# Graph attention in a network kernel: the value product also gives the weight sums, VectorE multiplies the edge counts in on the way out of PSUM, and GpSimd forms the exponential product

## Chip, cores and metric

One core of one Trainium2 chip. The metric is the device time of the kernel in microseconds (us), taken as the median of several runs. The profile shows one execution, instruction by instruction; its times are counted from the start of its span.

## What is computed

The reference applies eight blocks to 625 nodes of 512 features each. The change touches only the first, a graph attention with 8 heads of 64 features over 10,000 edges:

```python
score = s_src + s_dst + einsum(diff, a_dif) + einsum(abs(diff), a_abs) + einsum(hr_src * hr_dst, a_prd)
alpha = leaky_relu(score, negative_slope=0.2)
ex = exp(alpha.T - segment_max(alpha.T, src)[src])
att = ex / (segment_sum(ex, src)[src] + 1e-16)
out = segment_sum(att[:, :, None] * h_e[:, dst], src)      # one row per node, 8 heads x 64
x = x + out
```

The kernel treats the edges as a dense 625 x 625 matrix for each head. An entry that has several edges is weighed by their number (`CNT`), an entry without an edge by zero.

## The kernel before

The 625 nodes are 5 tiles of 125. The stage in question takes 5 tiles x 8 heads, so 40 heads `k = 8 t + h`, and for each it makes the 125 x 625 block of weights of the tile's source nodes against all nodes. Each engine has its own order of instructions, written out by hand, and semaphores tie them together. There are four buffers `SP0[k % 4]` for the block and four `BENT[k % 4]` for its second exponential; the PSUM tile `RAW` of raw scores and the PSUM tile `TURNED` exist once.

One head goes through these steps (names are functions of the program; one line number each, of the main instruction):

- `raw(k)`, TensorE (L946, L948): the raw scores into `RAW`, as a piece of 512 columns in one bank and one of 113 (114) in the next. It waits until VectorE has read `RAW` for head k-1.
- `raw_scores(k)`, VectorE (L2387): adds the edge term `TSC`, writes `SP0` and takes the row maximum. `shift(k)` (L2396, L2398) makes the biases of the exponentials of it.
- `bent(k)` (L1652) and `exp_scores(k)` (L1658, L1659), ScalarE: the leaky rectifier is split, so that the weight is the product of two exponentials, "slope" in `SP0` and "bend" in `BENT`.
- `counted(k)`, GpSimd (L1994): multiplies the slope exponential by `CNT`.
- `weighted(k)`, VectorE (L2406): multiplies by the bend exponential and sums each row, which gives the denominator.
- `turn_head(k)`, TensorE (L958): 5 transposes into `TURNED`. `turned_head(k)`, ScalarE (L1663): copies them to `PTS`.
- the value product, TensorE (L981): 5 fp32 matmuls (10 entries in the trace) of `PTS` with 64 columns of `HE`, into a PSUM slot "N" that holds all 8 heads of the tile.

TensorE's order in round k is `raw(k+4)`, `left` when k % 4 == 1 (L930: 8 matmuls that make the left factor of the next four heads, in a PSUM slot "T"), `turn_head(k+1)`, value product of head k. VectorE's is `left` when k % 4 == 3 (L2377), `raw_scores(k+4)`, `weighted(k+2)`, `shift(k+4)`, in the first rounds `merge` (L2308, L2309: two adds of 125 x 625 that complete `CNT` and `G` of a tile, at k = 1 and 6), and at h == 2 `add_heads(t-1)` for the tile before: denominator and reciprocal (L2414, L2415), multiply out of PSUM (L2417), add to X (L2422), statistics (L2099 to L2101), and the normalisation of the tile before that (L2106). Below, a round is the time from one `raw_scores` to the next.

SyncE loads the edge terms of tile t+1 (2.4 MB) into `TSC` once the tile t-1 has been read. After the last tile the normalised rows are turned (L735) and the next block starts (L996).

Of the kernel before, what the change touches and what calls it, by code (L numbers as in the profile page):

```python
# [21 lines left out]
N, E, D = 625, 10000, 512  # L22
P, NT = 125, 5
# [11 lines left out]
MAIN, TAIL = BANK, N - BANK  # L35
MAGIC = 12582912.0
# [148 lines left out]
def program(nc, a, out, loops):  # L185
# [6 lines left out]
    def passing(name, shape, dt=F32):  # L192

        with nc.sbuf_tensor(name, shape, dt) as t:
            return t
# [11 lines left out]
    with ctx:  # L207
# [20 lines left out]
        EA1 = passing("EA1", [DH0, N])  # L228
        CONDR = sb("CONDR", [128, N], F32R)
# [46 lines left out]
        HR_ = 5072  # L276
# [4 lines left out]
        with nc.sbuf_tensor("AR_hot", [128, 10192], F32):  # L281
            HOT1 = passing("HOT1", [128, NT, 4 * P], F32R)
# [21 lines left out]
        HE = XL  # L304
# [10 lines left out]
        IDB = [view(12696 + 1000 * b, 128, 2, 1000, dt=I16) for b in range(2)]  # L315
# [27 lines left out]
        SUMS_AT = [YF, AR[:, PT_:PT_ + 2500], AR[:, PT_ + 2500:PT_ + 5000], YF, YF]  # L343
# [23 lines left out]
        TSC = [view(at, P, N * HEADS0) for at in (HR_ + 2 * NT * D, PT_)]  # L367
# [3 lines left out]
        PTS = [view(HR_ + 2 * NT * D + 5000 + 625 * b, P, NT, P) for b in range(2)]  # L371
        SG = [view(PT_ + 625 * b, 128, N) for b in range(2)]
# [32 lines left out]
        RAW = PS[0:P, 2 * BANK:2 * BANK + N + 1]  # L405
# [35 lines left out]
        counted_ready = sem("counted_ready")  # L441
        heads_turned, heads_taken = sem("heads_turned"), sem("heads_taken")
        negmax_ready, exp_ready, sums_ready = sem("negmax_ready"), sem("exp_ready"), sem("sums_ready")
        weights_summed, prob_ready = sem("weights_summed"), sem("prob_ready")
# [20 lines left out]
        normed_before = []  # L465
# [229 lines left out]
        def _(pe):  # L695
# [81 lines left out]
            pe.wait_ge(start_done, 9)  # L777
# [182 lines left out]

# [5 lines left out]
            for k in range(4):  # L966
                raw(k)
            turn_head(0)
            for k in range(HEADS_ALL):
                h = k % HEADS0  # L970
                if k + 4 < HEADS_ALL:
                    raw(k + 4)
                if k % 4 == 1:
                    left((k + 7) // 4)
                if k + 1 < HEADS_ALL:
                    turn_head(k + 1)
                if h == 0:
                    o = fill("N")
                pe.wait_ge(heads_taken, k + 1)
                for c in range(NT):  # L980
                    last = mm(o.ap[0:P, DH0 * h:DH0 * (h + 1)], PTS[k % 2][:, c, :],  # L981
                              HE[:, c, DH0 * h:DH0 * (h + 1)], start=(c == 0), stop=(c == NT - 1))
                if h == HEADS0 - 1:
                    last.then_inc(o.filled, 1)
            pe.wait_ge(raw_taken, HEADS_ALL)
# [482 lines left out]
        def _(act):  # L1468
# [58 lines left out]
            act.wait_ge(start_done, 9)  # L1527
            act.wait_ge(keys_ready, 2)
            for t in range(NT):
                if t == NT - 1:  # L1530
                    psum.skip(T=ET // 4, W=STEPS - 1)
                    s = take("W")
                    fn(NODE_ROWS, s.ap[0:96, 0:N], ACT.Copy)
                    fn(VROW[:, :], s.ap[0:96, 0:N], ACT.Copy).then_inc(s.taken, 1)
                    act.wait_ge(s.taken, n.now(s.filled))
                    psum.skip(W=1)
                s = take("N")
                fn(HE[:, t, :], s.ap[0:P, :], ACT.Copy).then_inc(s.taken, 1)
                if t < 4:
                    apart(t)  # L1540
                    from_hot(t)
# [105 lines left out]
            def bent(k):  # L1647
                t, h = divmod(k, HEADS0)
                act.wait_ge(raw_taken, k + 1)
                if k >= 4:  # L1650
                    act.wait_ge(weights_summed, k - 3)
                fn(BENT[k % 4], SP0[k % 4], ACT.Relu, bias=U[:, t, h:h + 1]).then_inc(bent_ready, 1)  # L1652
# [21 lines left out]
            turned_head(0)  # L1674
            for k in range(HEADS_ALL):
                if k + 3 < HEADS_ALL:
                    exp_scores(k + 3)
                if k + 1 < HEADS_ALL:
                    turned_head(k + 1)
# [4 lines left out]
            psum.skip(N=NT)  # L1684
# [238 lines left out]
        def _(pool):  # L1923
# [12 lines left out]
            g.memset(SM[:, :], 0.0).then_inc(start_done, 1)  # L1936

# [52 lines left out]
            def counted(k):  # L1990
                if k % HEADS0 == 0:
                    pool.wait_ge(sums_merged, k // HEADS0 + 1)
# [3 lines left out]
            for k in range(3):  # L1996
                counted(k)
            for k in range(NT * HEADS0):
                t, h = divmod(k, HEADS0)
                if k + 3 < NT * HEADS0:  # L2000
                    counted(k + 3)
                if h == 2 and t:
                    inverse_roots([t - 1])
# [69 lines left out]
        def _(dve):  # L2073
# [65 lines left out]
            dve.wait_ge(start_done, 9)  # L2139
# [160 lines left out]
            dve.wait_ge(start_done, 9)  # L2300
# [100 lines left out]
            def weighted(k):  # L2401
                t, h = divmod(k, HEADS0)
                z = SP0[k % 4]
                dve.wait_ge(bend_ready, k + 1)
                dve.wait_ge(counted_ready, k + 1)
# [4 lines left out]
            def add_heads(t):  # L2410

                den = HM[:, t % 2, 3, :]
                dve.wait_ge(weights_summed, HEADS0 * (t + 1))
                step(v.tensor_scalar(den, HM[:, t % 2, 2, :], 1e-16, None, ALU.add))  # L2414
                step(v.reciprocal(den, den))  # L2415
                s, y = take("N"), Y[0:P, t, :]
                v.tensor_tensor(y.rearrange("p (h d) -> p h d", d=DH0),  # L2417
                                s.ap[0:P, :].rearrange("p (h d) -> p h d", d=DH0),
                                den.unsqueeze(2).broadcast_to([P, HEADS0, DH0]), ALU.mult)\
                 .then_inc(s.taken, 1)  # L2420
                dve.wait_ge(s.taken, n.now(s.filled))
                step(v.tensor_tensor(X[0:P, t, :], X[0:P, t, :], y, ALU.add))  # L2422
                stats(t, X[0:P, t, :])
                if t:
                    norm_y(t - 1)
# [11 lines left out]
            weighted(0)  # L2437
            weighted(1)
            for k in range(NT * HEADS0):
                t, h = divmod(k, HEADS0)  # L2440
                if k % 4 == 3:
                    left((k + 5) // 4)
                if k + 4 < NT * HEADS0:
                    raw_scores(k + 4)
                if k + 2 < NT * HEADS0:
                    weighted(k + 2)
                if k + 4 < NT * HEADS0:
                    shift(k + 4)
                if k in (1, 6):
                    merge(3 + k // 6)  # L2450
                if h == 2 and t:
                    add_heads(t - 1)
            add_heads(NT - 1)
# [571 lines left out]
```

## Time and profile before

| what | us |
|---|---|
| median of 3 runs (2321.63 to 2322.45) | 2321.89 |
| span of the profiled execution | 2314.6 |
| the attention stage in it, first `raw_scores` to the last value product | 173.3 |
| TensorE busy over the span | 2155.4 |
| VectorE busy over the span | 1043.3 |

The profiled execution's span ends with its last instruction; the 7.3 us between it and the median of the runs lie around it. PE is TensorE's matmul queue, PEld its weight loads, DVE VectorE, ACT ScalarE, POOL GpSimd, SP SyncE. A busy PE in the profile is not a PE at its peak: ends of matmuls are modelled, and neighbouring ones overlap, so the pace is read from starts. PEclk is the granted TensorE clock, 1.00 for 2.4 GHz and 0.50 for 1.2 GHz.

### The profile page before, as it was taken

What the parts mean: (1) busy time and instruction counts of PE and PEld (TensorE: products, weight loads), DVE (VectorE), ACT (ScalarE), POOL (GpSimd) and SP (SyncE); (2) the same over time, 40 slices, a digit from 0 to 9 for tenths busy, and PEclk for the clock granted to TensorE, in tenths of its full rate; (3) what the DMA queues carried; (4) which work ended last, traced back from release to release, by engine and by line L of the source; (5) the groups of instructions that cost most, each with busy time, mean ns of one, the idle gap of its engine ahead of it and who ended that gap; (6) DMA issues with size and microseconds to landing.
All of it is one profiled execution on the core that took longest, in us unless ns stands there. A gap on an engine that the chain in (4) does not pass through costs nothing.

```text
span 2314.6 us, 21913 instructions
## 1 busy us (share of the span) xinstructions
PE 2155.4 (93%) x8137; PEld 1248.1 (54%) x8137; DVE 1043.3 (45%) x2156; ACT 729.8 (32%) x1221; POOL 540.3 (23%) x457
## 2 busy tenths in 40 slices
PE   6899896888889999988999999999999999999998
PEld 3566563787445555444565565565555544444443
DVE  8897677886324332454454453453453410000002
ACT  1576555675421110003243243243242111111110
POOL 4677762332210000110202202202202200022202
PEclk9999998787999979998999999999999899999999
DMA  9522205431020110023101101101101577787832
GB/s 344 167 31 38 27 4 126 123 78 58 0 96 19 55 55 7 1 76 116 65 9 59 64 10 59 65 10 59 55 1 55 195 272 297 296 306 294 298 143 71
DMA packets 61507, 237.47 MB, mean 103 GB/s; under 512 B 23343, under 2 KB 28419, under 8 KB 39276
## 3 DMA queue, kind: packets, MB, share of 16 engines
q1 hardware_dynamic: 31898, 168.25, 20.3%
q0 software_dynamic: 26336, 62.19, 8.8%
q10 hardware_dynamic: 3168, 5.63, 0.7%
q8 instruction: 66, 1.08, 0.2%
q14 instruction: 39, 0.32, 0.0%
HBM read 204.06 MB, written 31.96 MB: 102 GB/s over the span
## 4 chain that ended last, share of the span: by engine, by line
PE 68%; DVE 11%; issue 8%; PEld 4%; ACT 3%; DMA 3%; POOL 3%; SPq 0%; PEldq 0%; ACTq 0%; DVEq 0%; POOLq 0%
PE PS L996 10%; PE PS L724 10%; PE PS L717 7%; PE PS L1387 7%; PE PS L1396 7%; PE PS L1425 6%; PE PS L868 3%; PE PS L1293 3%; PE PS L1034 2%; PE PS L1273 2%; PE PS L735 1%; DMA pair_scores<-TS,SIDX 1%; PEld PS L717 1%; DVE AR L2406 1%; POOL pair_scores L1971 1%
## 5 line engine op out<-in xcount | busy, mean ns | idle before, releaser
L1942 POOL TENSOR_TENSOR RSTD<-VE,HALF 125x1 f32<-125x1 f32 x100 | 81.7, 817 | 1017.3 <-DVE VE L2101 1017.3
L996 PE MATMUL PS<-XT,WR 128*128 128x500 f32 (+2 forms) x992 | 236.2, 396 | 8.4 <-ACT XT L1493 4.4
L868 PE MATMUL PS<-HR,HOT 125*125 125x512 f32 x800 | 212.8, 414 | 16.4 <-DVE HOT L2245 16.4
L724 PE MATMUL PS<-WR,XT 128*125 128x512 f32 (+1 forms) x464 | 208.0, 596 | 12.2 <-DVE AR L2696 7.7
L2911 DVE TENSOR_TENSOR AR<-AR,PS 128x512 f32<-128x512 f32 (+1 forms) x44 | 30.2, 687 | 404.9 <-PE PS L1396 404.9
L996 PEld LDWEIGHTS PS<-XT,WR 128*128 128x128 f32 x992 | 146.0, 194 | 89.2 <-issue 74.7
L868 PEld LDWEIGHTS PS<-HR,HOT 125*125 125x125 f32 x800 | 147.9, 193 | 58.5 <-DVE HOT L2245 16.8
L1960 POOL DMA_INDIRECT pair_sums<-CW,SIDX x80 | 136.2, 1703 | 56.3 <-DMA pair_sums<-CW,SIDX 24.5
L724 PEld LDWEIGHTS PS<-WR,XT 128*125 128x125 f32 x464 | 87.1, 194 | 101.4 <-issue 86.4
L717 PE MATMUL PS<-XT,WR 128*128 128x113 f32 (+3 forms) x432 | 127.5, 453 | 1.8 <-DVE CW L2209 1.3
L1902 ACT ACTIVATE AR<-PS 128x512 f32<-128x512 f32 (+1 forms) x44 | 26.3, 597 | 299.3 <-PE PS L1387 299.3
L2123 DVE TENSOR_TENSOR AR<-PS,AR 125x512 f32<-125x512 f32 x55 | 38.0, 691 | 178.7 <-PE PS L724 106.3
L717 PEld LDWEIGHTS PS<-XT,WR 128*128 128x128 f32 (+1 forms) x432 | 69.8, 196 | 65.3 <-issue 64.1
L1971 POOL DMA_INDIRECT pair_scores<-TS,SIDX x80 | 89.1, 1114 | 61.4 <-DMA pair_scores<-TS,SIDX 46.5
L1493 ACT ACTIVATE XT<-PS 128x500 f32<-128x500 f32 x60 | 35.4, 590 | 214.0 <-PE PS L735 214.0
L717 PE MATMUL PS<-AR 128*125 128x113 f32 (+3 forms) x360 | 102.4, 439 | 0.0
L1425 PE MATMUL PS<-AR,MODW 128*128 128x512 f32 (+1 forms) x192 | 86.4, 593 | 0.7 <-ACT MODW L1891 0.7
L1994 POOL TENSOR_TENSOR AR<-AR,CNT 125x625 f32<-125x625 f32 x40 | 56.8, 1419 | 104.9 <-ACT AR L1658 104.9
L717 PEld LDWEIGHTS PS<-AR 128*125 128x125 f32 (+1 forms) x360 | 57.3, 187 | 43.8 <-issue 43.6
L724 PE MATMUL PS<-WR,AR 128*125 128x512 f32 (+1 forms) x200 | 76.6, 530 | 1.7 <-ACT AR L1876 0.9
L2245 DVE SCALAR_TENSOR_TENSOR HOT<-AR,NODE,WR 125x500 fp32r<-125x500 int16 x100 | 71.2, 731 | 7.0 <-ACT WR L1525 6.0
L2266 DVE TENSOR_REDUCE TS<-WR 125x8 f32<-125x512 f32 x80 | 54.4, 680 | 42.1 <-DMA pair_scores<-TS,SIDX 42.1
(422 smaller groups left out, 3940.3 us busy)
## 6 DMA issues: line engine op xcount, KB each, us to landing
WR<-in_qkv SPq DMA_DIRECT2D x12, 1024.0 KB
WR<-in_omm SPq DMA_DIRECT2D x12, 1024.0 KB
pair_scores<-CNT SPq DMA_DIRECT2D x1, 12212.0 KB, 36.4
AR<-pair_scores SPq DMA_DIRECT2D x5, 2187.5 KB
AR<-in_x_a SPq DMA_DIRECT2D x10, 1024.0 KB, 9.8
AR<-in_x_b SPq DMA_DIRECT2D x10, 1024.0 KB, 4.9
AR<-in_x_c SPq DMA_DIRECT2D x10, 1024.0 KB, 7.2
WR<-in_x_a SPq DMA_DIRECT2D x8, 1024.0 KB, 8.9
```

The lines of the kernel that those rows point to most:

```text
L717: last = mm(s.ap[0:parts, c0:c1], lhs(k), rhs(k)[:, c0:c1], start=(k == 0), stop=(k == terms - 1))
L724: last = mm(s.ap[0:P, 0:cols], lhs, rhs, start=(k == 0), stop=(k == len(pairs) - 1))
L868: last = mm(DIFF[m % 4], HOT[g % 2][0:P, k, tile(j)], HR[0:P, k, :, b, :], start=(k == 0 and b == 0), stop=(k == NT - 1 and b == 1))
L996: last = mm(by_tile(s)[:, t0:t1, :], w[:, k, 128 * m:128 * (m + 1)], XT[:, k, P * t0:P * t1].rearrange("p (c n) -> p c n", n=P), start=(k ...
L1293: one = mm(main.ap[:, 0:MAIN], v_, PTH[h % 2][:, k, 0:MAIN], start=(k == 0), stop=(k == NT - 1))
L1387: last = mm(bank(2 + k % 2, rows_of(k)), stationary(k, c), w[:, c, :], start=(c == 0), stop=(c == K4 - 1))
L1396: last = mm(bank(4 + k % 2, rows_of(k)), stationary(k, c), w[:, c, :], start=(c == 0), stop=(c == K4 - 1))
L1425: last = mm(bank(6 + n % 2, rows), HTX[k % 2][:, c, 0:rows], w[:, c, :], start=(u == 0 and c == 0), stop=((is_shared(k) or u == 1) and c = ...
L1942: g.tensor_tensor(RSTD[:, t:t + 1], VE[:, t:t + 1], HALF[:, :], ALU.pow)\
L1960: g.indirect_dma_start(out=pair_sums[m % 2], out_offset=bass.IndirectOffsetOnAxis(ap=SIDX[:, m:m + 1], axis=0), in_=CW[:, m, :], in_offset ...
L1971: g.indirect_dma_start(out=pair_scores, out_offset=bass.IndirectOffsetOnAxis(ap=SIDX[:, m:m + 1], axis=0), in_=TS[:, m % SCORES_AHEAD, :], ...
L2245: v.scalar_tensor_tensor(HOT[g % 2][0:P, k, :], IDB[g // 2 % 2][0:P, 1, 500 * (g % 2):500 * (g % 2 + 1)], NODE[:, 0, k:k + 1], FROM[q % 4] ...
```

## The change

The row sum is taken out of VectorE's product: `HE` gets a 65th column of ones for each head, so that the value product returns the sum of the weights beside the 64 values. The count is multiplied in after the transposition: the count tile is turned once for each node tile (10 more PSUM slots "T" in all, 25 transposes on TensorE, 10 copies on ScalarE), and VectorE multiplies by it when it empties `TURNED`, where ScalarE copied before. GpSimd forms the product of the two exponentials. With 4 x 65 columns a head group fills half a tile, so a PSUM slot "N" now holds 4 heads and the division is made twice for each tile. The add to X goes to GpSimd (but for the last tile), statistics and normalisation of a tile move to later rounds (h == 5 and h == 7). `RAW` is cut at 314 instead of 512 columns. One more `memset` is made on GpSimd at the start.

```diff
-        HE = XL
+        HE = view(XL_, P, NT, HEADS0, DH0 + 1)
+        COUNTS_TURNED = [view(16480, P, NT, P), CTT.rearrange("p (c n) -> p c n", c=NT)]
-        RAW = PS[0:P, 2 * BANK:2 * BANK + N + 1]
+        RAW = PS[0:P, 3 * BANK - RAW_CUT:3 * BANK - RAW_CUT + N + 1]
...
-                for c0, c1 in ((0, MAIN), (MAIN, N)):
+                for c0, c1 in ((0, RAW_CUT), (RAW_CUT, N)):
             def turn_head(k):
-                pe.wait_ge(weights_summed, k + 1)
+                pe.wait_ge(head_weighed, k + 1)
+            def turn_counts(t):
+                if t >= NT:
+                    return
+                pe.wait_ge(sums_merged, t + 1)
+                for cs in ((0, 1, 2, 3), (4,)):
+                    s = fill("T")
+                    for c in cs:
+                        last = nc.tensor.transpose(s.ap[0:P, P * (c % 4):P * (c % 4 + 1)], CNT[:, t, tile(c)],
+                                                   ID[0:P, 0:P])
+                    last.then_inc(s.filled, 1)
+                if h == 3:
+                    turn_counts(k // HEADS0 + 1)
-                if h == 0:
+                if h % 4 == 0:
                     o = fill("N")
-                    last = mm(o.ap[0:P, DH0 * h:DH0 * (h + 1)], PTS[k % 2][:, c, :],
-                              HE[:, c, DH0 * h:DH0 * (h + 1)], start=(c == 0), stop=(c == NT - 1))
+                    last = mm(o.ap[0:P, (DH0 + 1) * (h % 4):(DH0 + 1) * (h % 4 + 1)], PTS[k % 2][:, c, :],
+                              HE[:, c, h, :], start=(c == 0), stop=(c == NT - 1))
...
-            def turned_head(k):
-                act.wait_ge(heads_turned, k + 1)
-                fn(PTS[k % 2], TURNED[:, :, 0:P], ACT.Copy).then_inc(heads_taken, 1)
+            def turned_counts(t):
+                if t >= NT:
+                    return
+                if t >= 2:
+                    act.wait_ge(heads_taken, HEADS0 * (t - 1))
+                s = take("T")
+                fn(COUNTS_TURNED[t % 2][:, 0:4, :], s.ap[0:P, 0:4 * P].rearrange("p (c n) -> p c n", c=4), ACT.Copy)\
+                    .then_inc(s.taken, 1)
+                s = take("T")
+                fn(COUNTS_TURNED[t % 2][:, 4, :], s.ap[0:P, 0:P], ACT.Copy).then_inc(s.taken, 1)
...
+                if k % HEADS0 == 4:
+                    turned_counts(k // HEADS0 + 1)
...
+            g.memset(HE[:, :, :, DH0:DH0 + 1], 1.0).then_inc(start_done, 1)
-                g.tensor_tensor(SP0[k % 4], SP0[k % 4], CNT[:, k // HEADS0, :], ALU.mult).then_inc(counted_ready, 1)
+                pool.wait_ge(bend_ready, k + 1)
+                g.tensor_tensor(SP0[k % 4], SP0[k % 4], BENT[k % 4], ALU.mult).then_inc(head_weighed, 1)
+            def add_heads(t):
+                for s, at in half_heads[2 * t:2 * t + 2]:
+                    pool.wait_ge(s.taken, at)
+                g.tensor_tensor(X[0:P, t, :], X[0:P, t, :], Y[0:P, t, :], ALU.add).then_inc(heads_added, 1)
...
-            def weighted(k):
-                v.tensor_tensor_reduce(out=z, in0=z, in1=BENT[k % 4], scale=1.0, scalar=0.0,
-                                       op0=ALU.mult, op1=ALU.add, accum_out=HM[:, t % 2, 2, h:h + 1])\
-                 .then_inc(weights_summed, 1)
+            def counted(k):
+                t, h = divmod(k, HEADS0)
+                if h == 0:
+                    for s, at in counts_at[t]:
+                        dve.wait_ge(s.taken, at)
+                dve.wait_ge(heads_turned, k + 1)
+                v.tensor_tensor(PTS[k % 2], TURNED[:, :, 0:P], COUNTS_TURNED[t % 2], ALU.mult)\
+                 .then_inc(heads_taken, 1)
+            def scale_heads(t, q):
+                s, den = take("N"), HM[:, t % 2, 2 + q, 0:4]
+                sums = s.ap[0:P, 0:4 * (DH0 + 1)].rearrange("p (h d) -> p h d", d=DH0 + 1)
+                step(v.tensor_scalar(den, sums[:, :, DH0], 1e-16, None, ALU.add))
+                step(v.reciprocal(den, den))
+                v.tensor_tensor(Y[0:P, t, 256 * q:256 * (q + 1)].rearrange("p (h d) -> p h d", d=DH0),
+                                sums[:, :, 0:DH0], den.unsqueeze(2).broadcast_to([P, 4, DH0]), ALU.mult)\
+                 .then_inc(s.taken, 1)
                 if k + 4 < NT * HEADS0:
                     raw_scores(k + 4)
-                if k + 2 < NT * HEADS0:
-                    weighted(k + 2)
+                if k + 1 < NT * HEADS0:
+                    counted(k + 1)
                 if k + 4 < NT * HEADS0:
                     shift(k + 4)
+                if h == 6:
+                    scale_heads(t, 0)
-                if h == 2 and t:
-                    add_heads(t - 1)
+                if h == 2 and t:
+                    scale_heads(t - 1, 1)
+                if h == 5 and t:
+                    dve.wait_ge(heads_added, t)
+                    stats(t - 1, X[0:P, t - 1, :])
+                if h == 7 and t > 1:
+                    norm_y(t - 2)
```

## Rows read from the trace of the kernel before

**Rows 1.** The page's first part: busy time of each engine.
```profile
PE 2155.4 (93%) x8137; PEld 1248.1 (54%) x8137; DVE 1043.3 (45%) x2156; ACT 729.8 (32%) x1221; POOL 540.3 (23%) x457
```

**Rows 2.** Windows: length; PE, PEld, DVE, ACT, POOL busy (instructions); PEclk, DMA share, GB/s.
```profile
394.80:413.30 18.50, 9.28 (x30) 7.20 (x31) 12.10 (x25) 9.18 (x13) 4.67 (x4) 0.50 0.84 214
413.30:443.10 29.80, 26.92 (x185) 24.57 (x186) 25.91 (x54) 22.82 (x34) 11.43 (x8) 0.89 0.69 173
443.10:476.70 33.60, 29.73 (x186) 27.44 (x185) 24.62 (x57) 23.65 (x34) 11.56 (x9) 0.80 0.30 75
476.70:509.80 33.10, 28.01 (x185) 25.70 (x186) 26.26 (x59) 23.67 (x35) 11.99 (x9) 0.85 0.29 76
509.80:540.30 30.50, 25.45 (x187) 23.23 (x186) 26.78 (x58) 23.63 (x34) 12.25 (x9) 0.89 0.01 2
540.30:553.70 13.40, 10.05 (x78) 8.99 (x77) 13.09 (x27) 10.51 (x15) 4.59 (x4) 0.97 0.24 83
553.70:568.10 14.40, 11.89 (x57) 11.89 (x58) 4.72 (x13) 4.30 (x6) 3.07 (x3) 0.50 0.38 154
```

**Rows 3.** The waits of the stage: us in total, times, longest.
```profile
PE PS L946 <- DVE HM L2387: 23.1, 11, 6.0
```

**Rows 4.** The timeline of two steady heads on VectorE and GpSimd: start, duration.
```profile
540.31 1.30 DVE L2387 CUSTOM_DVE_ANT_0 AR<-PS,AR 125x625 f32<-125x625 f32 x1
...
541.27 1.29 POOL L1994 TENSOR_TENSOR AR<-AR,CNT 125x625 f32<-125x625 f32 x1 [1.93 <-ACT AR L1658]
...
541.53 1.69 DVE L2406 CUSTOM_DVE_ANT_0 AR<-AR,MASK 125x625 f32<-125x625 f32 x1
...
543.16 0.21 DVE L2396 SCALAR_TENSOR_TENSOR SH<-SLOPES,HM,UP 125x2 f32<-125x2 f32 x1
...
543.52 1.29 DVE L2387 CUSTOM_DVE_ANT_0 AR<-PS,AR 125x625 f32<-125x625 f32 x1
```

**Rows 5.** Single lines over the whole run: ns min/median/max, first and last start.
```profile
L2387 DVE CUSTOM_DVE_ANT_0 AR<-PS,AR x40: 1261/1296/1319, 394.8 to 553.7; 125x625 f32<-125x625 f32 x40
L2406 DVE CUSTOM_DVE_ANT_0 AR<-AR x10: 1108/1469/1942, 408.2 to 548.2; 125x625 f32<-125x625 f32 x10
L1994 POOL TENSOR_TENSOR AR<-AR,CNT x40: 1285/1452/1896, 401.2 to 557.4; 125x625 f32<-125x625 f32 x40
L2487 DVE TENSOR_TENSOR AR<-AR,PS x2: 799/802/806, 587.6 to 836.9; 128x625 f32<-128x625 f32 x2
```

**Rows 6.** The timeline of TensorE over one head without a gap, clock 1.00.
```profile
478.20 0.71 PE L946 MATMUL PS<-HRT_HIGH,LEFT 128*125 128x512 f32 x2
...
479.18 1.11 PE L930 MATMUL PS<-HRT_LOW,WR 128*128 128x125 f32 x8
...
480.13 0.71 PE L958 MATMUL PS<-CS,AR 125*125 125x125 f32 x5
...
480.68 1.20 PE L981 MATMUL PS<-AR 125*125 125x64 f32 x10
...
481.69 0.47 PE L946 MATMUL PS<-HRT_HIGH,LEFT 128*125 128x512 f32 x1
```

**Rows 7.** The timeline of VectorE through one `add_heads`, up to the next `raw_scores`.
```profile
550.38 0.16 DVE L2414 TENSOR_SCALAR HM<-HM 125x8 f32<-125x8 f32 x1
...
550.82 0.69 DVE L2417 TENSOR_TENSOR Y<-PS,HM 125x512 f32<-125x512 f32 x1
...
552.26 0.69 DVE L2099 BATCH_NORM_STATS2 ST<-X 125x6 f32<-125x512 f32 x1
...
553.74 1.27 DVE L2387 CUSTOM_DVE_ANT_0 AR<-PS,AR 125x625 f32<-125x625 f32 x1
```

**Rows 8.** Windows of TensorE alone, around a gap: length, busy (instructions), PEclk, DMA share, GB/s.
```profile
438.20:441.80 3.60, 1.85 (x15) 1.00 0.04 7
441.80:445.20 3.40, 3.22 (x20) 0.76 0.01 2
```

**Rows 9.** The timeline of TensorE at clock 0.50.
```profile
557.42 2.20 PE L981 MATMUL PS<-AR 125*125 125x64 f32 x10
```

More of the change, by code:

```diff
@@ L35 @@
 MAIN, TAIL = BANK, N - BANK
+RAW_CUT = 314
 MAGIC = 12582912.0
@@ L228, in program @@
         EA1 = passing("EA1", [DH0, N])
+        CTT = passing("CTT", [P, N])[:, :]
         CONDR = sb("CONDR", [128, N], F32R)
@@ L280, in program @@
             HR = passing("HR", [128, NT, HEADS0, 2, DH0], F32R)
-        with nc.sbuf_tensor("AR_hot", [128, 10192], F32):
+        with nc.sbuf_tensor("AR_hot", [128, HR_ + 2 * NT * D], F32):
             HOT1 = passing("HOT1", [128, NT, 4 * P], F32R)
@@ L314, in program @@
         HOT = [HOT1, HOT0]
-        IDB = [view(12696 + 1000 * b, 128, 2, 1000, dt=I16) for b in range(2)]
+        IDB = [view(12724 + 1000 * b, 128, 2, 1000, dt=I16) for b in range(2)]
         APART = [view(16696 + 250 * b, P, 4 * P, dt=BF16) for b in range(4)]
@@ L366, in program @@
         WIDX = IDST_ROWS[:, 0:2 * SPARE].rearrange("p (u s) -> p u s", u=2)
-        TSC = [view(at, P, N * HEADS0) for at in (HR_ + 2 * NT * D, PT_)]
+        TSC = [view(at, P, N * HEADS0) for at in (HR_ + 2 * NT * D, HR_)]
         BENT = [view(PT_ + 12250, P, N), BENT_SPARE[:, :]] + [
@@ L967, in _ @@
                 raw(k)
+            turn_counts(0)
             turn_head(0)
@@ L980, in _ @@
                 for c in range(NT):
-                    last = mm(o.ap[0:P, DH0 * h:DH0 * (h + 1)], PTS[k % 2][:, c, :],
-                              HE[:, c, DH0 * h:DH0 * (h + 1)], start=(c == 0), stop=(c == NT - 1))
-                if h == HEADS0 - 1:
+                    last = mm(o.ap[0:P, (DH0 + 1) * (h % 4):(DH0 + 1) * (h % 4 + 1)], PTS[k % 2][:, c, :],
+                              HE[:, c, h, :], start=(c == 0), stop=(c == NT - 1))
+                if h % 4 == 3:
                     last.then_inc(o.filled, 1)
+                    half_heads.append((o, n.now(o.filled)))
             pe.wait_ge(raw_taken, HEADS_ALL)
@@ L1673, in _ @@
                     exp_scores(k - 1)
[L1674 removed]
+            turned_counts(0)
             for k in range(HEADS_ALL):
@@ L1988, in signed, with product @@
                     yield
-            def counted(k):
-                if k % HEADS0 == 0:
-                    pool.wait_ge(sums_merged, k // HEADS0 + 1)
+            def product(k):
                 pool.wait_ge(slope_ready, k + 1)
-                g.tensor_tensor(SP0[k % 4], SP0[k % 4], CNT[:, k // HEADS0, :], ALU.mult).then_inc(counted_ready, 1)
-            for k in range(3):
-                counted(k)
+                pool.wait_ge(bend_ready, k + 1)
[4 more added lines that the diff above has]
+                g.tensor_tensor(X[0:P, t, :], X[0:P, t, :], Y[0:P, t, :], ALU.add).then_inc(heads_added, 1)
             for k in range(NT * HEADS0):
                 t, h = divmod(k, HEADS0)
-                if k + 3 < NT * HEADS0:
-                    counted(k + 3)
-                if h == 2 and t:
-                    inverse_roots([t - 1])
+                product(k)
+                if h == 6 and t:
+                    add_heads(t - 1)
+                if h == 1 and t > 1:
+                    inverse_roots([t - 2])
+            inverse_roots([NT - 2])
             inverse_roots([NT - 1])
@@ L2399, in shift, with turned_counts @@
                 n.add(negmax_ready)
-            def weighted(k):
-                t, h = divmod(k, HEADS0)
-                z = SP0[k % 4]
-                dve.wait_ge(bend_ready, k + 1)
-                dve.wait_ge(counted_ready, k + 1)
-                v.tensor_tensor_reduce(out=z, in0=z, in1=BENT[k % 4], scale=1.0, scalar=0.0,
-                                       op0=ALU.mult, op1=ALU.add, accum_out=HM[:, t % 2, 2, h:h + 1])\
-                 .then_inc(weights_summed, 1)
[L2410 to L2414, printed above, removed]
+            counts_at = {}
+            def turned_counts(t):
+                if t < NT:
+                    counts_at[t] = [psum.next("T")[0:2] for _ in range(2)]
+            def counted(k):
+                t, h = divmod(k, HEADS0)
+                if h == 0:
[8 more added lines that the diff above has]
+                step(v.tensor_scalar(den, sums[:, :, DH0], 1e-16, None, ALU.add))
                 step(v.reciprocal(den, den))
[L2416 to L2419, printed above, removed]
+                v.tensor_tensor(Y[0:P, t, 256 * q:256 * (q + 1)].rearrange("p (h d) -> p h d", d=DH0),
+                                sums[:, :, 0:DH0], den.unsqueeze(2).broadcast_to([P, 4, DH0]), ALU.mult)\
                  .then_inc(s.taken, 1)
                 dve.wait_ge(s.taken, n.now(s.filled))
[L2422 to L2425, printed above, removed]
             left(0)
@@ L2436, in _ @@
                     merge(1 + k // 2)
-            weighted(0)
-            weighted(1)
+            turned_counts(0)
+            counted(0)
             for k in range(NT * HEADS0):
@@ L2450, in _ @@
                     merge(3 + k // 6)
+                if h == 4:
+                    turned_counts(t + 1)
+                if h == 6:
+                    scale_heads(t, 0)
                 if h == 2 and t:
-                    add_heads(t - 1)
-            add_heads(NT - 1)
+                    scale_heads(t - 1, 1)
[4 more added lines that the diff above has]
+                    norm_y(t - 2)
+            scale_heads(NT - 1, 1)
+            step(v.tensor_tensor(X[0:P, NT - 1, :], X[0:P, NT - 1, :], Y[0:P, NT - 1, :], ALU.add))
+            stats(NT - 1, X[0:P, NT - 1, :])
+            norm_y(NT - 2)
             norm_y(NT - 1)
```

26 lines of the change are left out of this document (12 added, 14 removed).

## The prediction

> **What bounds the kernel now.** I read the page first: TensorE is busy 93% of the span [rows 1]. That is an average over eight blocks, and the change lies in one, so I cut that stage into windows at the starts of `raw_scores` of heads 0, 4, 12, 20, 28, 36 and 39, and to the last value product [rows 2]. The reader is to see that no engine is full, that 8 heads take 29.8 to 33.6 us, and that the clock column never stands at 1.00: TensorE runs part of each stretch at 1.2 GHz, and all of the first and last.
>
> Next the waits. TensorE's longest class in the stage is `raw` on the reading of `RAW`, 23.1 us in 11 times, up to 6.0 [rows 3]. So VectorE holds TensorE, and the timeline shows with what. In a round VectorE starts `raw_scores` at 540.31, the product at 541.53, `shift` at 543.16 and the next `raw_scores` at 543.52 without a pause: 1.22 + 1.63 + 0.36 = 3.21 us [rows 4]. The product is the odd one. It has from 1.11 to 1.94 us on buffers of one kind, while `raw_scores`, of the same size, keeps to 1.26 to 1.32 in all 40 [rows 5]. The long one shown started while GpSimd's multiply ran (541.27 for 1.29) [rows 4], so half a microsecond of it is that neighbour.
>
> The Trainium skill (SBUF — State Buffer, Who interferes with whom) says that a VectorE instruction with two SBUF inputs contends with GpSimd's reads, and one with at most one SBUF input doesn't. The trace agrees: L2406 has two and stretches, L2387 reads PSUM and SBUF and doesn't [rows 5].
>
> TensorE's own work in a round is smaller. At clock 1.00, start to start: `raw` 0.98 (478.20 to 479.18), `left` 0.95, five transposes 0.55, value product 1.01 (480.68 to 481.69) [rows 6]. That is 2.54, and 3.49 with `left`. VectorE's `add_heads` adds 3.36 us (550.38 to 553.74) [rows 7], once a tile, in which TensorE runs dry. What a gap costs is seen in the clock: behind a stretch in which TensorE idled 1.75 of 3.60 us, the granted clock fell from 1.00 to a mean of 0.76, so to 1.2 GHz within that window [rows 8]. At 1.2 GHz the value product takes 2.20 instead of 1.20 [rows 6, 9].
>
> **VectorE's line after.** The product goes, and `counted` comes: PSUM times SBUF over 125 x 625, for which L2487 has 0.80 in both of its two instances [rows 5]. With one SBUF input it should keep that beside GpSimd, as L2387 does; bounds 0.74 (less the overlap of neighbours) and 1.30 (as L2387). I take 0.80, the same operation and size. A round is 1.22 + 0.80 + 0.36 = 2.38. On top, for a tile: `left` twice 0.6 (an estimate: 500 columns at the rate of L2487's 625). `add_heads` had 3.36: 0.44 small steps, 0.72 multiply and 0.72 add (550.82 to 552.26), 1.48 statistics and normalisation [rows 7]. Now 0.85 at h = 2 and at h = 6 (0.44 and half the multiply, bounds 0.80 and 1.16), 1.0 at h = 5, 0.5 at h = 7. The add goes to GpSimd.
>
> **TensorE's line after.** `raw` has the same columns, cut 314 and 311 instead of 512 and 113. The three matmuls of a short piece take nearly as long as weight loads allow; I take 0.85 for 0.98, bounds 0.78 and 0.98, since no row has this shape. The transposes stay 0.55. The value product has 65 columns for 64: 1.02, bounds 1.01 and, if the odd width went at the slower rate of rows 9, 2.2. A round: 2.42, 3.37 with `left`. Turning the counts adds 0.55 at h = 3. `left` at h = 5 needs a "T" slot that ScalarE empties only after `bent(k+4)` at h = 4, about 0.5 later; queued behind it on TensorE is `turn_head`, for which `counted` and then the statistics wait, so that round loses up to 0.9.
>
> **A tile of 8 rounds at clock 1.00.** `RAW` exists once, so neither engine gets ahead, and each round is the longer of the two lines. From h = 0: 2.42 (TensorE), 3.37 (TensorE, `left`), 2.38 + 0.85 + 0.6 = 3.8 (VectorE), 2.97 (TensorE, counts), 2.42, 3.37 + 0.9 = 4.3, 3.8 (VectorE), 2.9 (VectorE, norm). Sum 26.0. Without the slot wait and with `raw` at 0.78 it is 24.7; with `raw` at 0.98 and 0.1 us of signalling in each round, 27.6. The old line gives 8 x 3.21 + 1.2 + 3.36 = 30.2 by the same method, against 30.5 measured [rows 2], which is why I trust it.
>
> **The others are covered.** GpSimd has 8 products at 1.29 to 1.90 [rows 5], one add and one power: under 17 of 26 us. That the product waits for both exponentials costs nothing: `shift(k)` is made 3 rounds before `turn_head(k)` wants it, about 9 us, and two exponentials (0.8 each allowed; ScalarE's mean instruction is 23.65 / 34 = 0.70 [rows 2]) and the product need under 4. ScalarE loses 8 copies a tile and gains 2, from 23.7 busy [rows 2]. Loading the edge terms is a DMA share of 0.29 to 0.30 over 33 us [rows 2], 10 us asked for a whole tile ahead. SyncE's and GpSimd's waits keep their order: GpSimd's add waits for the second division, made at h = 2, and VectorE wants it at h = 5; the power for tile t-2 stands behind statistics made three rounds before. The `memset` at the start writes 40 elements in each of 125 partitions while the first loads are under way, and I cost it at nothing (at most the 0.16 of L2414, as small an operation [rows 7]).
>
> **The sum, stretch by stretch** (before from rows 2):
> - Head 0 to 4, 18.5: the first transposes wait for GpSimd's product instead of for VectorE's, which took up to 1.94 [rows 5] and stood behind `merge` (two operations of 0.80). The counts take about 1 us back, `raw` at half clock gives 0.3 twice. -3.5 (bounds -1.5, -4).
> - Head 4 to 12, 29.8: half clock to begin with, no statistics yet, and `merge` with a division and `left` in two adjoining rounds. I take 28.1 (27 to 30): -1.7.
> - Head 12 to 20, 33.6: that last gap is as deep as the one of rows 8, so I let the clock fall once, 7 us with half of the work, less 0.8 of slack: 26.0 + 2.7 = 28.7: -4.9.
> - Head 20 to 28, 33.1: 26.0, -7.1. Head 28 to 36, 30.5: -4.5. Head 36 to 39, 13.4: 2.42 + 2.42 + 3.2 = 8.0 (no more `left`), -5.4. In all these TensorE's gaps are at most 3.8 - 2.42 = 1.4 us, where `add_heads` made one of over 3, so I let the clock stay up.
> - Head 39 to the last product, 14.4 at clock 0.50, TensorE busy 11.9 of it. At 1.00 the four remaining heads are a chain of `raw_scores` 1.3, `counted` 0.8, `shift` 0.4, two exponentials 1.6, product 1.4, transposes 0.6, statistics and `counted` 1.1, product 1.0 = 8.2: -6.2 (0 if the clock is down).
> - The end: the denominator is now made after the last product, not before: +0.4. The add stays where it was.
>
> Sum: -3.5 - 1.7 - 4.9 - 7.1 - 4.5 - 5.4 - 6.2 + 0.4 = -32.9. The span goes from 2314.6 to 2281.7 and, with the 7.3 us around it, the median of the runs from 2321.9 to 2289. Later blocks move as they are: their loads wait on this stage's semaphores, not on time.
>
> **Rivals.** (A) *The clock goes on falling in each tile.* For it: rounds h = 2 and h = 6 leave TensorE a gap of 1.4 us, not far below the 1.75 behind which it fell [rows 8]. Against it: from 540.3 to 553.7 TensorE idled 3.35 us in many small gaps, and the clock's mean was 0.97 [rows 2]. Price: 2.7 in each of three stretches and the 6.2 of the end, so 2289 + 14 = 2303.
>
> (B) *GpSimd's product stands on the path*, the lead of three rounds being used up by ScalarE's order. Then each round pays what GpSimd takes more than VectorE, 1.45 - 0.80 = 0.65 [rows 5]: 40 x 0.65 = 26, so 2315. For it: GpSimd now waits for both exponentials. Against it: 17 us of work in 26, and the lead above. The Trainium skill (GPSIMD Engine Reference, 4.1 Engine selection) warns of this move: a two-input elementwise operation is about twice as slow there as on VectorE. The trace agrees with the ratio, 1.8.
>
> (C) *Slower: TensorE never gets out of 1.2 GHz.* A round there is twice 0.85 + 0.55 + 1.01, so 4.8, and 5.4 with `left` and counts spread out; my sum has (173.3 - 32.9) / 40 = 3.5. From 33 / 1.9 = 17 such rounds beyond mine on, the gain is gone; all 40 would make the stage 216 us instead of 173, so 2365. For it: the first 18.5 us are at 0.50, and the change adds TensorE work but takes none of the gap at the start away. Against it: between heads 4 and 12 the clock rose to a mean of 0.89 with TensorE busy all but 2.9 us [rows 2], and there it will be no less busy.
>
> (D) *It doesn't do what it says*: VectorE's gain turns into equal waits for TensorE, 2322.
>
> **Chances.** Forecast 0.66, A 0.22, B 0.04, C 0.05, D 0.03. The forecast's own range: 24.7 to 27.6 a tile is -5 to +6 over 3.7 tiles, the start and end add -1 to +3, and TensorE may come warmer into the next block (-3, since it starts at 0.50 now): 2280 to 2298. The odd width at the slow rate of rows 9 (1.2 a round, 2336) gets no more than 1 in 100, out of C's share. With most of A, 2278 to 2304. What this kernel's measurement can tell from no change is 0.2%, 4.6 us. Faster by more: forecast, A, B and a little of the rest, 0.92. Within: 0.03. Slower: 0.05.
>
> **What would show it.** Right: VectorE's L2406 gone and a multiply from PSUM of 0.80 without spread; starts of `raw_scores` 2.4 to 3.8 apart; PEclk 1.00 from head 20 on; TensorE's waits on `RAW` under 1.5 us each; 26 us for 8 heads; last value product about 33 us earlier. Wrong: the value product above 1.1 us, gaps in front of the transposes whose releaser is GpSimd, a clock that falls once a tile, or 'T' slots holding TensorE at h = 5 for more than 0.5.

## The result, and the profile after

The changed kernel takes 2303.16 us (median of 4 runs, 2298.93 to 2305.86) against 2321.76 for the kernel before: a ratio of 0.9928, with a 95% interval of 0.9904 to 0.9953. It is faster by about 0.7%, where 1.4% (2289) was forecast. By the ratio it stands at 2305, a microsecond past 2304, where the wider range of the prediction ends, and past the 2298 of the forecast's own. One execution of all those below, of the changed kernel with `RAW` cut at 512, took 2518.78 us at a mean granted clock of 0.83, where its others had 0.96, and is left out of its median and ratio.

First the same cut as in [rows 2]: the windows of the stage, at the starts of `raw_scores` of heads 0, 4, 12, 20, 28, 36 and 39. Columns: length; PE, PEld, DVE, ACT, POOL busy (instructions); PEclk; DMA share; GB/s.

```profile
398.40:413.30 14.90, 9.45 (x34) 7.79 (x34) 10.76 (x23) 8.97 (x14) 4.09 (x3) 0.52 0.75 192
413.30:444.40 31.10, 26.73 (x190) 25.79 (x191) 24.39 (x50) 19.68 (x28) 10.80 (x8) 0.88 0.74 193
444.40:472.20 27.80, 24.40 (x192) 23.51 (x191) 24.83 (x51) 19.50 (x29) 12.58 (x10) 0.96 0.36 91
472.20:503.60 31.40, 28.06 (x193) 27.29 (x192) 25.72 (x52) 20.05 (x29) 12.54 (x10) 0.84 0.32 81
503.60:533.20 29.60, 26.35 (x191) 25.61 (x190) 25.36 (x53) 19.88 (x29) 12.52 (x10) 0.88 0.00 1
533.20:543.40 10.20, 9.49 (x77) 8.93 (x75) 10.03 (x19) 7.20 (x10) 4.09 (x3) 1.00 0.05 9
543.40:558.00 14.60, 12.39 (x60) 12.42 (x61) 7.53 (x19) 3.18 (x5) 4.36 (x4) 0.58 0.54 221
```

The reader is to see two things. The stage has 159.6 us instead of 173.3, where 140.4 was forecast: the first stretch came out as worked out (14.9 against 15.0), but the four stretches of 8 heads, forecast at 28.1, 28.7, 26.0 and 26.0, take 31.1, 27.8, 31.4 and 29.6, and the last two, forecast at 8.0 and 8.2, take 10.2 and 14.6. The largest single miss is the last, where the clock is down. And VectorE is busy 25.4 of 29.6 us, though it lost its long product. The stage also starts later, at 398.4 instead of 394.8. In the profiles of this study that start lies anywhere between 392.9 and 400.4, in variants of the changed kernel alone, so I take it for no part of the change.

Where VectorE's time is, the timeline of VectorE and GpSimd over two rounds shows: start, duration, in brackets the idle time before it. L2445 is `counted`, L2427 and L2429 are `shift`, L2020 is GpSimd's product.

```profile
508.16 1.29 POOL L2020 TENSOR_TENSOR AR<-AR 125x625 f32<-125x625 f32 x1 [1.91 <-ACT AR L1678]
508.36 1.10 DVE L2427 SCALAR_TENSOR_TENSOR SH<-SLOPES,HM,UP 125x2 f32<-125x2 f32 x1
...
509.49 0.15 DVE L2429 TENSOR_SCALAR SH<-SH 125x1 f32<-125x1 f32 x1
...
510.84 0.79 DVE L2445 TENSOR_TENSOR AR<-PS,CTT 125x625 f32<-125x625 f32 x1
...
511.35 1.52 POOL L2020 TENSOR_TENSOR AR<-AR,BENT_SPARE 125x625 f32<-125x625 f32 x1 [1.91 <-ACT BENT_SPARE L1678]
...
511.56 1.32 DVE L2427 SCALAR_TENSOR_TENSOR SH<-SLOPES,HM,UP 125x2 f32<-125x2 f32 x1
```

An operation on two numbers in each partition takes 1.10 and 1.32 us, and it ends when GpSimd's product ends: 508.36 + 1.10 = 509.46 beside 508.16 + 1.29 = 509.45, and 512.88 beside 512.87. `counted`, which GpSimd's product overlaps too at 511.35, keeps its 0.79. The timeline of all 40 heads says the same. In 26 of them a GpSimd instruction (23 products, 3 adds to X) runs when the operation starts, and each time the operation ends 0.00 to 0.03 us behind it; the 14 that meet none take 0.20 to 0.22. Over all heads, from the views of the single lines (ns min/median/max, first and last start):

```profile
L2427 DVE SCALAR_TENSOR_TENSOR SH<-SLOPES,HM,UP x40: 198/350/1329, 399.7 to 545.4; 125x2 f32<-125x2 f32 x40
...
L2445 DVE TENSOR_TENSOR AR<-PS,CTT x16: 793/806/811, 442.6 to 527.9; 125x625 f32<-125x625 f32 x16
...
L2020 POOL TENSOR_TENSOR AR<-AR,MASK x20: 1288/1292/1296, 412.0 to 547.6; 125x625 f32<-125x625 f32 x20
...
L2020 POOL TENSOR_TENSOR AR<-AR,BENT_SPARE x10: 1510/1520/1537, 408.7 to 541.0; 125x625 f32<-125x625 f32 x10
```

In the kernel before, this operation (L2396 there) took 206 to 227 ns in all 40, and none of the 40 overlapped a GpSimd instruction: in [rows 4] the multiply ends at 542.56 and shift starts at 543.16. In the windows of that line alone it now has 22.1 us in all, 13.7 more than 40 x 0.21. `counted` is at 0.80, as forecast, and GpSimd's product has lost the long cases that L1994 had [rows 5].

TensorE has a new wait. The view of L972, the transposes of the counts, and one of its instances in the timeline:

```profile
L972 PE MATMUL PS<-CS,CNT x25: 270/273/417, 408.0 to 514.6; 125*125 125x125 f32 x25
its engine sat idle before it (us, times) until:
  DVE LEFT L2408: 12.5, 8
```

```profile
513.84 0.68 DVE L2408 TENSOR_TENSOR LEFT<-PS,LEFT 128x500 fp32r<-128x500 f32 x1
514.44 1.28 DVE L2418 CUSTOM_DVE_ANT_0 AR<-PS,AR 125x625 f32<-125x625 f32 x1
514.58 0.37 PE L972 MATMUL PS<-CS,CNT 125*125 125x125 f32 x1 [2.06 <-DVE LEFT L2408]
```

The fifth transpose at h == 3 needs the "T" slot that `left` filled at h == 1, and VectorE empties it only behind `raw_scores`, `counted`, `shift` and the division. The 12.5 us add up both of TensorE's queues, so they are about half that in time, up to 2.06 us at once. `turn_head` is queued behind. The wait was 1.24 us in heads 12 to 20 and 2.06 in each of the next two stretches, and right behind both of those the clock fell. Windows of TensorE alone, in the changed kernel and, for comparison, in the one with the counts turned a round later, which waits at another place:

```profile
480.00:484.00 4.00, 1.94 (x15) 1.00 0.00 0
484.00:494.40 10.40, 10.40 (x50) 0.51 0.93 238
```

```profile
484.00:488.00 4.00, 1.80 (x18) 1.00 0.00 0
488.00:494.40 6.40, 6.07 (x50) 1.00 0.93 250
```

The first pair has a fall behind 2.06 us of idle time (4.00 - 1.94), the second has none behind 2.20. So the length of such a gap alone doesn't decide, and what does isn't shown here.

### The profile page after: what moved, and what is told of

It is laid out like the page before. It is cut to its first block, busy times and chain, and to the rows that moved or that the text cites. A ratio compares the mean times of both kernels' runs of the same rounds, so it can differ in the third digit from the quotient of the medians.

```text
span 2304.0 us, 21929 instructions
## 1 busy us (share of the span) xinstructions
PE 2150.1 (93%) x8162; PEld 1249.8 (54%) x8162; DVE 1039.0 (45%) x2127; ACT 710.8 (31%) x1191; POOL 542.1 (24%) x462
## 4 chain that ended last, share of the span: by engine, by line
PE 68%; DVE 11%; issue 7%; PEld 4%; ACT 3%; POOL 3%; DMA 3%; SPq 0%; ACTq 0%; PEldq 0%; DVEq 0%; POOLq 0%
PE PS L727 10%; PE PS L1015 10%; PE PS L720 7%; PE PS L1406 7%; PE PS L1415 7%; PE PS L1444 6%; PE PS L1312 3%; PE PS L871 3%; PE PS L1053 2%; PE PS L1292 2%; DVE AR L2418 1%; PE PS L738 1%; PEld PS L720 1%; DMA pair_scores<-TS,SIDX 1%; POOL pair_scores L1998 1%
## 5 line engine op out<-in xcount | busy, mean ns | idle before, releaser
L1444 PE MATMUL PS<-WR,MODW 128*128 128x512 f32 (+1 forms) x160 | 71.9, 592 | 0.0
```

The lines of the kernel that those rows point to most:

```text
L1444: last = mm(bank(6 + n % 2, rows), HTX[k % 2][:, c, 0:rows], w[:, c, :], start=(u == 0 and c == 0), stop=((is_shared(k) or u == 1) and c = ...
```

## The experiments

All are compared in two ways: by the runs, and by the profiled stage, here from the first `raw_scores` to the start of the last matmul of the value products. That is 172.8 us before and 158.5 after (both end within 1.2 us of the windows' edges). A stage is that of one execution, with its clock; the runs are medians of 4 to 12. In the expectations, "Theory S" says that the missing gain went into shift, and "Theory T" that TensorE's waits for slots and its falling clock set the rounds.

**Shift with one SBUF tensor.** The edit:

```diff
-                step(v.scalar_tensor_tensor(z, SLOPES[:, :], HM[:, t % 2, 0, h:h + 1], UP[:, t, h, :],
-                                            ALU.mult, ALU.add))
+                m = HM[:, t % 2, 0, h:h + 1]
+                step(v.tensor_scalar(z[:, 1:2], m, -0.8, UP[:, t, h, 1:2], ALU.mult, ALU.add))
+                v.tensor_scalar(z[:, 0:1], m, -0.2, None, ALU.mult)
```

> The changed kernel with shift(k) rewritten so that no VectorE operation in it reads two tensors from SBUF: three small tensor_scalar operations instead of one scalar_tensor_tensor and one tensor_scalar. Theory S (the gain that is missing went into shift: its first operation took 22.1 us in 40 instances instead of 40 x 0.21 = 8.4, because it reads two SBUF tensors while GpSimd's product runs): no small operation over 0.25 us, the stage from the first raw_scores to the last value product falls from 159.6 us to 146 to 152, the run from 2303 to 2291 to 2297. Rival T (the rounds are TensorE's: its waits for PSUM slots and a clock that falls set them, and VectorE's delay only fills waits): the small operations get short, but VectorE then waits for TensorE, stage 157 to 160, run 2300 to 2304.

Measured: 2294.04 us, ratio to before 0.9889 (0.9873 to 0.9905); stage 145.4 us. Its three operations, and the windows of three tiles (heads 12 to 20, 20 to 28, 28 to 36):

```profile
L2428 DVE TENSOR_SCALAR SH<-HM,UP x40: 195/204/215, 397.5 to 530.8; 125x1 f32<-125x1 f32 x40
...
L2429 DVE TENSOR_SCALAR SH<-HM x40: 153/154/155, 397.7 to 531.0; 125x1 f32<-125x1 f32 x40
...
L2430 DVE TENSOR_SCALAR SH<-SH x40: 142/144/146, 397.8 to 531.1; 125x1 f32<-125x1 f32 x40
```

```profile
440.40:469.00 28.60, 26.22 (x191) 25.29 (x191) 22.46 (x59) 19.62 (x29) 12.56 (x10) 0.89 0.36 88
469.00:494.90 25.90, 23.52 (x193) 22.64 (x193) 22.86 (x61) 19.96 (x29) 12.53 (x10) 1.00 0.38 98
494.90:520.70 25.80, 23.43 (x191) 22.42 (x190) 22.77 (x61) 19.75 (x29) 12.54 (x10) 1.00 0.00 1
```

One operation more, and VectorE is busy 2.4 to 2.9 us less a tile. The rounds shrink, the clock stays at 1.00 in both later tiles, and the tile has the forecast's 26 us. From h = 0 the rounds of heads 20 to 28 are 2.5, 3.4, 3.8, 3.1, 2.5, 4.1, 3.8 and 2.7, where the forecast had 2.4, 3.4, 3.8, 3.0, 2.4, 4.3, 3.8 and 2.9; in the changed kernel they are 2.9, 3.2, 4.8, 4.8, 4.6, 4.5, 3.8 and 2.7, the middle ones at the lower clock. TensorE's wait in front of L972 also shrinks, to 1.00 us in each of the three later tiles. The stage loses 13.1 us. That this is about what shift had grown by is chance, since the clock's falls are in it too; heads 36 to 39, at clock 1.00 in both profiles, go from 10.2 to 8.2. Theory S holds; the rival, by which VectorE's delay only filled waits, falls.

**Is it GpSimd's reading, or shift itself?** The changed kernel with shift as the change left it, and GpSimd's product cut to 8 columns, so that it leaves out most of the second exponential and its output is another one:

```diff
-                g.tensor_tensor(SP0[k % 4], SP0[k % 4], BENT[k % 4], ALU.mult).then_inc(head_weighed, 1)
+                g.tensor_tensor(SP0[k % 4][:, 0:8], SP0[k % 4][:, 0:8], BENT[k % 4][:, 0:8], ALU.mult).then_inc(head_weighed, 1)
```

> The changed kernel with shift as it was, and GpSimd's product cut to 8 of the 625 columns (the rest of the weights keeps the slope exponential alone, so the output is another one; the order of instructions and all waits stay). Theory S (shift is lengthened by GpSimd reading SBUF at that time): shift's first operation back at 0.21 us in all 40 instances, stage as in the run with one SBUF tensor, 145 us, within 3. Rival W (shift is long for a reason of its own, such as its place behind counted and the accumulator read): still 0.35 in the median and up to 1.3, stage about 158.

Measured: 2292.40 us, ratio 0.9865 (0.9848 to 0.9883); stage 143.9 us. The same line as above, now:

```profile
L2427 DVE SCALAR_TENSOR_TENSOR SH<-SLOPES,HM,UP x40: 202/210/440, 401.3 to 533.8; 125x2 f32<-125x2 f32 x40
```

The instruction, its place and its waits are the same, only its neighbour is short: 0.21 us in the median. The longest, 0.44, is beside GpSimd's add to X, which is still whole, and ends with it (534.24 beside 534.23):

```profile
532.96 1.27 POOL L2025 TENSOR_TENSOR X<-X,Y 125x512 f32<-125x512 f32 x1
...
533.80 0.44 DVE L2427 SCALAR_TENSOR_TENSOR SH<-SLOPES,HM,UP 125x2 f32<-125x2 f32 x1
```

So it is the neighbour. And cutting GpSimd's product from 1.29 to 0.20 us brings the stage only 1.5 us below the version whose shift avoids the contention, and the two ratios overlap: GpSimd's product is hardly on the path otherwise.

**Counts turned a round later.** Alone, and with the first edit:

```diff
-                if h == 3:
+                if h == 4:
                     turn_counts(k // HEADS0 + 1)
```

> The changed kernel with the turning of the next tile's counts on TensorE one round later (h == 4 instead of h == 3), when VectorE has already emptied the PSUM slot T of left. Theory T: the 12.5 us that TensorE waits in front of these transposes (up to 2.1 us at a time) go, the clock falls less often, stage 159.6 to 150 to 155, run 2303 to 2294 to 2299. Theory S: that wait lies beside VectorE's shift, division and left, which set this round anyway, so the wait only moves; stage 157 to 160, run 2300 to 2303.

> Both edits together: shift with one SBUF tensor, counts turned at h == 4. If S and T each hold a part: stage 142 to 148 us, run 2285 to 2292. If S alone: as e1. If the clock still falls once a tile behind the gap of the rounds with division and left, PEclk below 0.9 in the tiles 2 and 3 and stage not below 148.

Measured alone: 2301.13 us, ratio 0.9914 (0.9901 to 0.9927), stage 154.3 us. The stage fits theory T and the run theory S, so neither expectation held whole; the runs don't separate this version from the changed kernel. Shift's first operation got worse there, 762 ns in the median and 27.4 us in all: VectorE comes to it at another time, and meets GpSimd more often. Measured together: 2281.69 us, ratio 0.9830 (0.9817 to 0.9844), and in a second set of runs 2280.15 and 0.9832 (0.9807 to 0.9856), with stages of 140.7 and 140.4; the first time both lie a little below the expected ranges, which begin at 2285 and 142. The first profile of both together, heads 12 to 20, 20 to 28, 28 to 36, 36 to 39 and the end:

```profile
445.10:473.40 28.30, 26.01 (x191) 25.39 (x190) 22.43 (x59) 19.85 (x29) 12.56 (x10) 0.88 0.35 89
473.40:498.80 25.40, 23.12 (x194) 22.55 (x193) 22.79 (x60) 20.07 (x29) 12.54 (x10) 1.00 0.39 100
498.80:524.20 25.40, 23.11 (x193) 22.41 (x192) 22.84 (x62) 19.95 (x29) 12.55 (x10) 1.00 0.00 1
524.20:532.30 8.10, 8.10 (x70) 7.92 (x68) 7.70 (x22) 7.16 (x10) 4.11 (x3) 1.00 0.01 2
532.30:540.80 8.50, 7.22 (x64) 6.99 (x64) 6.70 (x16) 3.16 (x5) 4.36 (x4) 1.00 0.93 370
```

The stage is 140.7 us, and no idle time stands in front of L972 any more. Set beside the forecast's stretches of 28.7, 26.0, 26.0, 8.0 and 8.2 these are its numbers, nearly one by one.

What each edit is worth by itself is best read in heads 20 to 39, where the clock was at 1.00 in all three versions. They take 59.9 us with shift rewritten, 65.9 with the counts moved and 58.9 with both. So at an unchanged clock the shift is worth 7.0 us in 19 heads (less than it grew by, since part of it lay beside TensorE's work), and the slot 1.0. The changed kernel has 71.3 there, with its two falls. In these profiles either edit kept those away. The end ran at clock 1.00 with both edits and at 0.62 and 0.63 with one, but also at 1.00 with neither when `RAW` was cut at 512 (the next experiment), so the edits alone don't decide that. In the stages of single profiles the two gains seem to add (13.1 and 4.2 beside 17.8 for both), but in the runs they don't: 9 and 2 us alone, 21 together, 10 us more than the sum where the intervals allow about 8. How much of that is the clock's isn't shown.

**The cut of RAW.** Undone in the changed kernel, and made alone in the kernel before:

```diff
-RAW_CUT = 314
+RAW_CUT = 512
```

> The changed kernel with RAW cut at 512 columns again, as before the change. Theory S (VectorE sets most rounds): raw on TensorE takes 0.98 instead of 0.85 us, but only in the 3 of 8 rounds that TensorE sets, so plus 0 to 2 us. Rival T: all 40 rounds, plus 4 to 6 us.

> The kernel before with only RAW cut at 314 instead of 512 columns. If VectorE sets its rounds (its product beside GpSimd's multiply), the shorter raw only lengthens TensorE's waits: within 2 us of before. If TensorE's work matters in the rounds at 1.2 GHz (10 to 12 rounds, 0.3 us each at that clock): 3 to 4 us faster.

Undone in the changed kernel: 2304.85 us, ratio 0.9935 (0.9915 to 0.9955), which overlaps the changed kernel's; its stage was even 3.6 us shorter, 154.9, its last stretch (8.4 us against 13.4) having run at clock 1.00. Nothing can be read from it on the cut. It repeats the clock's falls, though: the wait in front of L972 was 1.00, 1.87 and 1.87 us, and the clock fell right behind the last two. Alone in the kernel before: 2315.47 us, ratio 0.9971 (0.9960 to 0.9982), so 6 us faster, more than either theory said, with a stage of 166.7. The profile has the rounds at clock 1.00 as they were (2.68, 3.21, 3.45), and shorter stretches where the clock was down. That the cut moved the clock's falls is what one profile suggests; it isn't shown.

**Shift rewritten in the kernel before.**

> The kernel before with only shift rewritten to one SBUF tensor. Theory S says that there VectorE's long product takes GpSimd's whole time on itself, so shift behind it is already at 0.21: nothing to gain, one more small operation a round costs 0.1, so 0 to plus 4 us. If the rewriting helps by itself (shorter small operations), 3 us or more faster than before.

Measured: 2318.07 us, ratio 0.9985 (0.9973 to 0.9997), stage 169.6. I had 0 to plus 4, and it is 3 us faster; the interval leaves out 1.0 by little, and the difference lies inside this kernel's 0.2%. The steady rounds are 0.05 us longer (3.26, 3.51), as the extra operation costs, and again there are fewer rounds at the lower clock. What stands is the size: the edit that gave the changed kernel 9 us (0.39%) gives the old one about a third of that (0.15%, at most 0.27% by the interval).

**VectorE's work moved into TensorE's rounds.** Both edits, and:

```diff
-                if h == 6:
+                if h == (5 if t else 6):
                     scale_heads(t, 0)
-                if h == 2 and t:
+                if h == 1 and t:
                     scale_heads(t - 1, 1)
-                if h == 5 and t:
+                if h == 4 and t:
                     dve.wait_ge(heads_added, t)
```

> Both edits of e3, and VectorE's per-tile work moved to the rounds that TensorE sets: the divisions at h == 1 and h == 5 instead of 2 and 6 (for tile 0 at 6 still), the statistics at h == 4, GpSimd's add one product earlier. By the rule that a round is the longer of the two engines' lines: h1 stays 3.4, h2 falls from 3.77 to 3.1, h4 rises from 2.9 to 3.4, h5 falls from 3.65 to 3.4, h6 from 3.77 to 3.1, so 25.4 to 24.2 a tile, 4 to 5 us faster than e3, about 2277. If lines don't combine that way (a late PSUM slot, or the add not ready), within 1 us of e3.

> e3 once more, beside e8 once more on the same chip, since their runs spread by more than the 6 us between their stages. The first raw_scores has started anywhere from 392.9 to 400.4 us in the profiles so far, and that is outside the change. Theory S: median 2280 to 2286, stage 139 to 143 us.

> e8 once more. If a round is the longer of two lines, the stage is 133 to 137 us again and the median 3 to 6 us below that of e9. If the blocks behind the stage take the gain back, stage 133 to 137 but median within 2 us of e9.

The rounds of the last full tile came out at 2.5, 3.5, 3.3, 2.7, 3.4, 3.2, 3.3, 2.7, together 24.4 us against 25.4: the rule held for each within 0.25 us. But the runs don't show it: 2283.26 us (0.9829, 0.9809 to 0.9848) where 2277 was expected, and in the second set 2280.56 (0.9832, 0.9809 to 0.9855) against 2280.15 for both edits alone, where 3 to 6 us less were expected. The two profiles of this one program say why it can't be seen in so few runs. Heads 12 to 20, first profile and second profile:

```profile
445.50:469.70 24.20, 22.94 (x191) 22.34 (x190) 22.37 (x59) 19.81 (x29) 12.57 (x10) 1.00 0.43 104
```

```profile
445.50:473.50 28.00, 26.73 (x191) 26.08 (x191) 22.40 (x60) 19.19 (x28) 12.55 (x10) 0.86 0.37 90
```

The same instructions, once with the clock at 1.00 throughout and once with a fall, 3.8 us apart; the stage was 134.8 and 139.1, the second outside the 133 to 137 that was expected in either case. I can't call this version faster than the one with both edits.

**And the cut once more**, in that version:

> e8 with RAW cut at 512 columns. Now TensorE sets five to six of eight rounds, so raw's 0.98 against 0.85 us must show in those: 24.4 us a tile becomes 25.0 to 25.2, the stage 137 to 139, the median 3 to 4 us above e10. If weight loads set raw in both cuts, no difference.

Measured: 2283.98 us, ratio 0.9841 (0.9817 to 0.9864), stage 135.3 where 137 to 139 was expected. The runs, 3.4 us above those of the version without it, don't separate the two. The tiles at clock 1.00 have 24.8 and 24.7 instead of 24.4 us. TensorE's rounds grew from 3.47 to 3.57 and from 2.50 to 2.55: the cut is worth 0.05 to 0.1 us in a round that TensorE sets, about half of what I gave it, and nothing in the others.

## Why the prediction was wrong, point by point

- **The step that failed** is in "VectorE's line after": "A round is 1.22 + 0.80 + 0.36 = 2.38." The 0.36 of shift was read in the old kernel, where shift stood behind the product, and the product had waited GpSimd out: in the 28 heads in which it overlapped GpSimd's multiply it ended 0.65 to 0.68 us behind that, and in the 12 others it took 0.80 to 0.82 us by itself, no more than `counted`. So nearly all that the exchange of the two could save on VectorE was this waiting, where the prediction put half a microsecond down to it. I had just cited the rule that an operation with two SBUF inputs contends, and applied it to the operation that went and the one that came, not to the one that stayed. `scalar_tensor_tensor` reads `SLOPES` and `UP` from SBUF. With the product gone it was next in line: 13.7 us in 40 heads, and when it was taken out the kernel was 9 us faster and its stage 13.1 us shorter, 7 us in 19 heads at an unchanged clock. The contention was not removed but handed on.
- **The slot at h == 3** was the smaller miss: "Turning the counts adds 0.55 at h = 3". I looked at the slot wait of `left` at h = 5 and not at the same wait here, up to 2.06 us. Undone it gave 1.0 us in 19 heads at an unchanged clock, beside what the clock's falls behind it cost. At h = 5, where the prediction allowed 0.9 for a slot, TensorE waited about 0.3.
- **The clock** came out as in rival A (falls at 0.84 and 0.88, the end at 0.58), and A's number, 2303, is the measured one. That the number fits is partly luck, since A had the rounds at their forecast length, and they were longer. Its reason doesn't hold as it stands: it blamed the gaps of h = 2 and h = 6. These are there in the version with both edits too, which runs at 1.00 from head 20 to the end, in two profiles out of two. The four falls in heads 20 to 36 of the changed kernel and of its version with `RAW` cut at 512 all came right behind a slot wait of 1.87 to 2.06 us; from head 12 on, none of the eight waits of 0.94 to 1.24 in these two, with shift rewritten and with the 8-column product had one behind it. But the version with the counts moved has gaps of 2.20 us at h = 2 and no fall. So in these profiles the falls go with the two misses, and by what rule stays open. The end, at 0.58, is 6.4 us of the stage's miss of 19.2.
- **Right**: the form of the argument. A round is the longer of the two engines' lines, and with both misses mended the tile is 25.4 us against 26.0, the end 8.5 against 8.2, the stage 140.7 against 140.4, the runs 2280 to 2282 against 2289 (why they gain more than the stage isn't shown). `counted` at 0.80, the first stretch at 14.9, ScalarE and GpSimd covered, the value product with 65 columns as fast as with 64 (1.02 us from 449.31 to the next step at 450.33, as forecast).
- **Mis-sized**: `raw` at 0.85. From its start to that of the next step it has 0.92 (508.37 to 509.29), so the cut saved half of what I took. The trust in the sum was put too high: it was tested on one old tile, the 30.5, while the other two beside it had 33.6 and 33.1.
- **Rival B** (GpSimd on the path) fell with the 8-column product, and TensorE waited for GpSimd's product once in the stage, 2.1 us. The ratio of 1.8 lies between two: on most buffers it is 1.29 to 0.80, so 1.6, on one kind 1.52 to 0.80, so 1.9. **C** and **D** didn't occur, and the first stretch shows that the start became no slower.

## What to carry to other kernels

When an instruction that absorbs a contention is removed, ask which instruction next to it would now meet the same neighbour, however small: here an operation on two numbers in each partition took up to 1.33 us, as long as one on 625. Apply a contention rule to every instruction that stays on that engine, not only to those in the diff. A duration read behind a long instruction may be short only because of it.

## What the runs showed of the hardware that I had not expected

- VectorE's `scalar_tensor_tensor` with two SBUF tensors of 125 x 2 ended with the GpSimd instruction that was running in all 26 cases, 0.00 to 0.03 us behind it (1.10 and 1.32 us in two of them, instead of 0.21). The `tensor_scalar` that takes one SBUF tensor and one SBUF scalar for each partition (L2428 above) stayed at 195 to 215 ns in all 40, most of them beside a GpSimd instruction: the scalar doesn't count as the second tensor. The Trainium skill (SBUF — State Buffer, Who interferes with whom) says that a VectorE instruction with two SBUF inputs contends with a GpSimd instruction that reads SBUF. The trace agrees, down to an operation of this size, which waits out the whole of the neighbour.
- One program, run twice, had the granted clock at 1.00 and at a mean of 0.86 over the same 8 heads, 24.2 and 28.0 us. Differences of that size in a single profile prove nothing in this stage, unless the clock is the same on both sides.
